# SyncE in place of GpSimd waits for the last gathers and scatters of the expert block

## The reference, cut to what matters

```
x = x + attn(experts1(x, cond))        # 2048 tokens of 256, this change lies between the two
x = x + ffn(adaln_attention(x, mask, cond))

experts1: gate = softmax(rmsnorm(x) @ wg + wg_b + cond @ gg + gg_b); top 2 of 8 experts per token
          out  = sum over the 2 experts of  weight_e * (relu(relu(x@W1_e+b1_e)@W2_e+b2_e)@W3_e+b3_e)
attn:     elu linear attention on that sum, layer norm, gated feed forward, layer norm
adaln_attention, ffn: causal softmax attention with 16 heads, then 16 small experts (8 of 16) and a shared one
```

## Time and profile before

| | us |
|---|---|
| median of 3 runs | 1006.46 |
| the runs | 1005.03 to 1008.07 |
| the profiled execution, its own time | 1007.15 |
| its span (first to last instruction) | 1005.4 |
| PE, DVE, ACT, POOL busy in it | 881.4, 738.4, 406.7, 406.6 |

### The profile page before, as it was taken

One profiled execution on the slowest core, in us unless ns is written; L12 is line 12 of the kernel. 1 busy time (PEld: TensorE's weight loads), 2 busy tenths in 40 slices (PEclk: granted clock), 3 DMA queues, 4 the chain that ended last, 5 costly groups with the idle time before them and its releaser, 6 DMA issues. The chain is left out here.

```text
span 1005.4 us, 17919 instructions
## 1 busy us (share of the span) xinstructions
PE 881.4 (88%) x5607; PEld 750.9 (75%) x5616; DVE 738.4 (73%) x1456; ACT 406.7 (40%) x779; POOL 406.6 (40%) x480
## 2 busy tenths in 40 slices
PE   4399999999956885699997889888899999999997
PEld 1299999999955675587796655446588888888886
DVE  5888888888835788768867866449667676767676
ACT  5356666666615543413336255578311111111110
POOL 3167777777742003076415532300233333333332
PEclk9599999999986997899998899999999999999999
DMA  7336313135125000140006910001001010101002
GB/s 269 105 96 208 104 44 126 43 125 182 43 72 184 1 1 0 42 160 1 1 1 107 179 41 2 1 1 33 1 17 32 16 31 16 31 16 31 16 0 84
DMA packets 50300, 61.81 MB, mean 61 GB/s; under 512 B 8014, under 2 KB 37768, under 8 KB 50248
## 3 DMA queue, kind: packets, MB, share of 16 engines
q1 hardware_dynamic: 43464, 43.85, 13.9%
q0 software_dynamic: 6336, 17.31, 7.2%
q10 hardware_dynamic: 448, 0.01, 0.0%
HBM read 47.26 MB, written 7.60 MB: 55 GB/s over the span
## 5 line engine op out<-in xcount | busy, mean ns | idle before, releaser
L2174 POOL TENSOR_TENSOR kTh<-at_acc,kTh 128x512 fp32r<-128x512 f32 x68 | 88.3, 1299 | 255.6 <-DVE kTh L2347 255.6
L2100 ACT ACTIVATE at_acc<-psum 128x512 f32<-128x512 f32 x68 | 40.8, 601 | 240.2 <-PE psum L1897 240.2
L2429 DVE SCALAR_TENSOR_TENSOR y<-psum,at_pT,y 128x256 f32<-128x256 f32 x272 | 112.2, 475 | 0.0
L1939 PE MATMUL psum<-at_wkh,kTh 128*128 128x256 f32 x544 | 106.6, 280 | 3.0 <-DVE y L2429 3.0
L1897 PE MATMUL psum<-act_hi,at_wkh 128*128 128x512 f32 x272 | 108.9, 400 | 0.3 <-ACT at_acc L2100 0.3
L1897 PE MATMUL psum<-act_hi,at_wkl 128*128 128x512 f32 x272 | 108.1, 398 | 0.0
L1897 PE MATMUL psum<-act_lo,at_wkh 128*128 128x512 f32 x272 | 108.1, 398 | 0.0
L441 ACT ACTIVATE e_u<-psum,e_bias 128x256 f32<-128x256 f32 x152 | 63.7, 472 | 96.4 <-PE psum L345 87.5
L2344 DVE TENSOR_TENSOR at_acc<-psum,at_acc 128x512 f32<-128x512 f32 x68 | 47.0, 692 | 74.7 <-PE psum L1897 61.4
L1939 PEld LDWEIGHTS psum<-at_wkh,kTh 128*128 128x128 f32 x544 | 87.9, 188 | 7.0 <-DVE y L2429 3.0
L1939 PE MATMUL psum<-at_wkl,kTh 128*128 128x256 f32 x272 | 75.9, 279 | 0.0
(11 more groups left out here) (513 smaller groups left out, 2813.8 us busy)
## 6 DMA issues: line engine op xcount, KB each, us to landing
e_raw<-in_W SPq DMA_DIRECT2D x16, 512.0 KB, 6.6
e_raw<-in_W SPq DMA_DIRECT2D x8, 1024.0 KB, 5.8
y<-in_x SPq DMA_DIRECT2D x4, 512.0 KB, 9.7
v_tok<-in_xT SPq DMA_DIRECT2D x4, 512.0 KB, 8.2
y<-y_rows SPq DMA_DIRECT2D x4, 512.0 KB, 7.9
v_tok<-y_rows SPq DMA_DIRECT2D x4, 512.0 KB, 8.8
v_tok<-in_x SPq DMA_DIRECT2D x4, 512.0 KB, 9.1
e_raw<-in_w_gate SPq DMA_DIRECT2D x16, 128.0 KB, 2.1
```

What stands on the lines that cost most here:

```text
L1939: last = pe.matmul(ps[4 + j][:, 0:D], hh[a][:, s % HS, j * P:(j + 1) * P], e2_w[par][b][:, OD:OD + D], start=n == 0, stop=n == 2)
L2100: act.activation(sl_sb[:, s % 2, :], ps[s % 2][:, :], ACT.Silu).then_inc(esil, 1)
L2174: pool.tensor_tensor(hh[1][:, s % HS, :], h32[:, s % 2, :], hh[0][:, s % HS, :], ALU.subtract).then_inc(hsp, 1)
L2429: dve.scalar_tensor_tensor(out=y[:, i, :], in0=ps[4 + j][:, 0:D], scalar=comb[:, i, bass.ds(2 * t + out_s // G, 1)], in1=y[:, i, :], op0=A ...
```

## The change

After the gathers and scatters of the last tile GpSimd waited for both semaphores to be full. These two waits are gone. SyncE, which had the wait for the scatters already, gets the one for the gathers ahead of it.

```diff
@@ SyncE, end of the expert block
                     total = first_tile(sp, E1 - 1) + sp.value_load(tiles[0:1, 0, E1 - 1:E1], min_val=1, max_val=T // ET)
+                    sp.wait_ge(xin, (total + 2) * (16 * TT))
                     sp.wait_ge(stored, (total + 2) * (16 * TT))
                     load_rows(sp, 0, held, gathered)
@@ GpSimd, end of the expert block
                     n = experts(pool, step)
                     take_dest(n, 2 * n + 1, TT)
-                    pool.wait_ge(xin, (n + 2) * (16 * TT))
-                    pool.wait_ge(stored, (n + 2) * (16 * TT))
```

## The result

The changed kernel takes 1002.8 us, the median of 11 runs (1000.55 to 1004.83), against 1006.42 us (1003.72 to 1008.07, 11 runs) for the kernel before on the same chip. The ratio is 0.9968 with the interval [0.9957, 0.9978]: 3.6 us faster where 1.7 were forecast (1004.8), at the low end of the range of 1002.8 to 1007.2, and hardly on the faster side of the 0.3% that a measurement can tell. The profiled execution took 1004.22 us.

The account below looks back on a forecast made before the run. TensorE is busy 88% of the span; GpSimd's drain holds the expert block's barrier. Starting it earlier gives -1.7 us, the moved wait and clock 0: median 1006.46 becomes 1004.8 us, range 1002.8 to 1007.2.

Parts of the forecast that it names:

- The mechanism: At the expert block's end, GpSimd's drain starts its work at the last scatter's record, opening the barrier 1.7 us earlier.
- Who opens the barrier: At the expert block's end, GpSimd's drain ends last and releases the others; SyncE was there 6 us earlier.
- What the drain works on: GpSimd's drain at the block's end costs 0.08 us per DMA issued since its last drain, landed or not: 6.94 us.
- The size of the shift: Barrier after the last scatter's issue: some 8.1 us, not 9.7; 1.7 us gained, ScalarE's idle time 14.9 us.
- The cap: Behind the barrier, ScalarE's load of rows lands at 302.5, limiting the gain to 2.0 us even with a free drain.
- The wait on SyncE: The gathers' wait moved to SyncE, ahead of its scatter wait, is already met and costs 0.
- The landing first: Drain at the block's end must first see the last scatter land; gain only some 0.3 us, 1006.2 us; chance 0.17.
- The fixed end: Drain's end hangs on the last scatter's issue, not the drain's start, so stays at 304.3: 1006.5 us; chance 0.08.
- The second pass: Drain finds a scatter unfinished and repeats its work, 5.3 us later: 1011.8 us; chance 0.07 shared with a costlier clock.
- The higher clock: TensorE isn't slowed behind the shorter pause before the next stage, 2.6 us more gained: 1002.2 us; chance 0.08.
- my lower bound: TensorE's clock behind the pause rises at the same moment as before, giving back at most 0.85 us of the gain.
- the granted clock: I take nothing: TensorE's clock behind the barrier was counted as 0, with -0.85 and +2.6 us kept for the range.

Follow-up runs that it names:

- the first job: The changed kernel's first measurement, 11 runs against the kernel before on the same chip: 1002.8 us, ratio 0.9968.
- the fifth experiment: Changed kernel plus 24 small DMAs on GpSimd at the start of the expert block, landed long before its end: ratio 0.9992 against the kernel before.
- The half that contains it: Against the kernel before, only the gathers' wait moved from GpSimd to SyncE, the scatters' wait kept on both: ratio 0.9995.
- the delay of 5: Changed kernel plus five chained memsets on GpSimd between the last scatter and the drain: ratio 0.9994 against the kernel before.
- 2.4 in the second: The changed kernel measured again without edit, 6 runs beside the kernel before on one chip: 1001.78 us, ratio 0.9959.
- 0.3 in the third: The changed kernel measured a third time without edit, 12 runs: 1004.56 us, ratio 0.9981 against the kernel before.

## Why the prediction was right, and what it left out

The mechanism and its size were right, 1.68 us of 1.7. That the median of the first job, 1002.8, still fell on the end of the range was luck: of its 3.6 us, 1.9 are no part of that mechanism.

**Who opens the barrier.** Right. GpSimd's drain ended last in every kernel that had the whole account in it there. Only with drains in the loop, where two DMAs were left for it, did SyncE come last.

**What the drain works on.** 6.94 us from the last scatter's record for 84 DMAs, as said; 8.90 for 108; 0.41 for 4 in the loop; 6.96 for the 84 when they are paid behind the barrier. The drain's record reads 8.32 us and not 7.9, since it begins at 294.76, 0.39 us ahead of the scatter's own start; what lies behind the scatter is what was forecast. The price of 0.08 us for each DMA, old ones too, taken from two stages, held for a third count within 0.002 us. It is not the whole account: a drain also waits for what is in flight. Here that is over first.

The Trainium skill (PSUM — Partial Sum Buffer, Engine vs sequencer instructions) says that a drain waits for the engine to be fully idle. By its records GpSimd ran nothing in the 8.90 us that the drain took behind the last scatter, and the 24 DMAs of the fifth experiment had landed some 270 us before; each still cost the drain 0.082 us. The trace doesn't show what the engine does in that time.

**The size of the shift.** 1.7 forecast, 1.68 measured; barrier 8.1 forecast, 8.06 measured. The idle time of ScalarE came out at 15.18 and not 14.9, and that figure alone would have misled, since it also counts when the engine fell idle.

**The cap.** 2.0 us by the landing of the rows: measured 2.0 in the two kernels without the drain in that place.

**The wait on SyncE.** 0 forecast. With two waits in a row, the one for the scatters (line 278) is now an instruction of its own, of 17 ns at the scatter's landing.

```profile
L278 SPq EVENT_SEMAPHORE  x1: 17/17/17, 297.6 to 297.6; - x1
```

The half that contains it makes -0.19 ± 0.38 us.

**The rivals.** The landing first: as the place where the list starts it is refuted by the 6.94 us from the scatter's record; as a second condition of the drain's end it is true, and hidden here. The fixed end: refuted by the same number and by the delay of 5. The second pass: a drain of 8.3 us, and 15 was its sign. The higher clock: it was described as full speed in the stretch of the earlier trace rows. The windows of the changed kernel that answer to it:

```profile
304.60:311.70 7.10, 5.30 (x16) 4.18 (x17) 2.33 (x5) 4.55 (x7) 2.93 (x5) 0.50 1.00 328
311.70:318.60 6.90, 6.14 (x22) 4.58 (x22) 5.41 (x8) 4.16 (x9) 3.43 (x2) 0.83 1.04 323
```

0.50 as before, and then 0.83 in place of 0.99: the same 22 matmuls are busy 1.1 us longer (6.14 against 5.07). A mean of 0.83 over 6.9 us is 0.34 x 6.9 = 2.3 us at half clock, so the rise came at 314.0, 1.1 us later than before on this clock, though the work began 1.2 earlier. That cost more than my lower bound, which had the rise at the same moment: 1.07 us of TensorE's time and not 0.85. The gain in the clock came after that and was larger, in this execution.

**The term that was mis-sized.** It is "the granted clock: I take nothing", with -0.85 and +2.6 as ends. What the kernel gained beyond the 1.68 us of the barrier is 1.4 ± 0.35 us over all 29 runs, 1.7 in the first job, 2.4 in the second and 0.3 in the third; the fit gives the clock 1.2 (0.43 x 2.7), 2.0, 2.0 and 0.1 of these. I had looked only at the stretch just behind the pause and asked whether the rise comes earlier; the granted clock of this kernel varies in all of the stage behind it and in the later ones too. The forecast's 1004.8 and the measured 1002.8 differ by that term, as far as the fit goes. Part of it is chance or the chip, since the same code gave +4.7 and +0.3 thousandths in different jobs. Whether a lasting part of it comes from the change stays open: 0.9541 against 0.9514 over all runs says so weakly, since it rests on the first two jobs, and no experiment here shows a way by which it would, beyond the shorter pause.

## What to carry to other kernels

A drain of GpSimd ahead of a barrier cost, in every such drain of these runs, 0.1 us and 0.08 for each DMA that this engine had issued since its last drain, or until its last DMA had landed if that was later: count them, and let no wait of that engine stand between its last DMA and the drain that another engine already does. Ask also what comes next in line before the drain is made cheaper still; here the landing of a load capped it 0.3 us further on. And for an edit worth 0.2%, measure its stretch from an event just ahead of it, since the time of the whole kernel moved by as much again with the granted clock, from job to job, with the same code.

## What the runs showed of the hardware that was not expected

- A drain of GpSimd waits for its DMAs in flight as well: with only two scatters on its list it ended 0.1 us behind the landing of the last, 1.6 us behind its record; five of the loop's drains ended 0.2 us behind a landing, up to 4.6 us behind the engine's last operation.
- A drain that is left out is not always paid later: the one of the semaphores' clearing took 0.35 us in the place where an explicit one took 7.14.
- Between kernels and jobs, a thousandth of mean granted clock went with 0.43 us of some 1005, and means of 6 to 12 runs of one and the same kernel, each against before in its own job, differed by 2.1 us (-4.12 and -1.97).
